# Unread bf16 products in TensorE's stream of a two-layer attention and expert kernel

## The reference, cut to what matters

```python
x = x + xattn_L0(layernorm(x), ctx)   # 16 heads of 8: causal self attention plus cross attention, projected
x = x + ffn_L0(layernorm(x))          # 8 experts of 128 -> 512 -> 128, relu, softmax over the best two
x = x + xattn_L1(layernorm(x), ctx)   # one head of 128, cross
x = x + ffn_L1(layernorm(x))          # 16 heads of 64; values and outputs mixed from the best two of 8 projections
```

## Time and profile before

| | |
|---|---|
| three runs, median | 1280.1 us (1278.98 to 1280.35) |
| profiled execution, its own time | 1274.52 us |
| its span, first to last instruction | 1272.8 us |
| mean granted TensorE clock over the span | 0.855 |
| instructions | 21333 |
| TensorE matmuls | 8499, busy 1118.9 us |

### The profile page before, as it was taken

How to read it: one execution, slowest core, us unless ns; L and a number is a source line. 1 busy time by engine, 2 the same in 40 slices (tenths; PEclk the granted TensorE clock), 3 DMA queues, 4 the chain that set the end, 5 groups by cost and what they waited for, 6 DMA issues and landing times.

```text
span 1272.8 us, 21333 instructions
## 1 busy us (share of the span) xinstructions
PE 1118.9 (88%) x8499; PEld 874.8 (69%) x8499; DVE 700.1 (55%) x1867; ACT 491.0 (39%) x1022; POOL 82.8 (7%) x246
## 2 busy tenths in 40 slices
PE   5888879899989998999989988998989998984696
PEld 4547645787569765887578855986678766873475
DVE  5503474856576565746575666657475657515400
ACT  4233406352434525352534434462536253422120
POOL 0020001000100001000100011000100010000000
PEclk8557958899889979898889978998889988998556
DMA  8000001051301421042103321052105220143322
GB/s 220 1 1 5 1 1 36 5 81 42 68 5 30 71 55 41 11 74 68 40 5 62 48 68 19 13 80 63 36 5 83 58 48 1 31 78 80 56 44 54
DMA packets 198033, 56.86 MB, mean 45 GB/s; under 512 B 173568, under 2 KB 193838, under 8 KB 197934
## 3 DMA queue, kind: packets, MB, share of 16 engines
q1 hardware_dynamic: 195630, 51.20, 20.6%
q10 hardware_dynamic: 2304, 4.29, 1.1%
HBM read 31.36 MB, written 24.12 MB: 44 GB/s over the span
## 4 chain that ended last, share of the span: by engine, by line
PE 74%; DVE 12%; ACT 7%; issue 2%; SPq 2%; DMA 2%; ACTq 0%; DVEq 0%
PE bank L737 10%; PE bank L928 10%; PE bank L773 9%; PE bank L843 5%; PE bank L884 5%; PE bank L663 4%; PE bank L624 3%; PE bank L678 3%; DVE negmax L1265 3%; PE bank L911 3%; ACT pa L1022 2%; PE bank L588 2%; PE bank L942 2%; ACT hi_part L1008 2%; PE bank L832 2%
## 5 line engine op out<-in xcount | busy, mean ns | idle before, releaser
L1265 DVE TENSOR_REDUCE negmax<-bank 128x2 f32<-128x512 f32 (+1 forms) x224 | 139.0, 683 | 57.2 <-PE bank L624 35.0
L1022 ACT ACTIVATE pa<-bank 128x512 f32<-128x512 f32 x224 | 123.4, 596 | 111.6 <-PE bank L678 73.7
L1039 ACT ACTIVATE pa<-bank,b_c 128x256 f32<-128x256 f32 x256 | 107.5, 471 | 117.9 <-PE bank L737 115.8
L737 PE MATMUL bank<-xnT_a,w 128*128 128x256 f32 x512 | 141.8, 429 | 0.1
L928 PEld LDWEIGHTS bank<-vb,pb 128*128 128x128 f32 x1024 | 129.6, 209 | 7.8 <-ACT pb L1101 3.0
L928 PE MATMUL bank<-vb,pb 128*128 128x65 f32 x1024 | 133.8, 294 | 1.2 <-ACT pb L1101 0.8
L773 PE MATMUL bank<-w,pa 128*128 128x128 f32 x1024 | 124.2, 276 | 0.0
L773 PEld LDWEIGHTS bank<-w,pa 128*128 128x128 f32 x1024 | 121.9, 192 | 3.2
L737 PEld LDWEIGHTS bank<-xnT_a,w 128*128 128x128 f32 x512 | 107.0, 219 | 18.4 <-ACT pa L1039 0.7
L1101 ACT ACTIVATE pb<-bank 128x512 f32<-128x512 f32 x128 | 69.8, 599 | 111.8 <-PE bank L888 110.9
L1419 DVE TENSOR_REDUCE negc<-bank 128x2 f32<-128x512 f32 x128 | 80.0, 684 | 46.4 <-PE bank L860 46.1
(11 more groups left out here) (239 smaller groups left out, 1690.5 us busy)
## 6 DMA issues: line engine op xcount, KB each, us to landing
v_d<-at SPq DMA_DIRECT2D x32, 256.0 KB, 3.3
vb<-v_d SPq DMA_DIRECT2D x32, 256.0 KB, 5.3
at_d<-at SPq DMA_DIRECT2D x32, 256.0 KB, 2.1
at<-at_d SPq DMA_DIRECT2D x32, 256.0 KB, 4.4
pv_d<-pvs SPq DMA_DIRECT2D x8, 512.0 KB, 2.8
pvs<-pv_d SPq DMA_DIRECT2D x16, 256.0 KB, 4.2
w<-in_L_ffn_W_dram ACTq DMA_DIRECT2D x1, 2048.0 KB, 10.5
bd<-mix_d SPq DMA_DIRECT2D x128, 8.0 KB
```

The lines of the kernel that those rows point to most:

```text
L737: mm = pe.matmul(BA[u % 2][:, c * T:(c + 1) * T], w1[:, e, f:f + P], xnT_a[:, :], start=True, stop=True)
L1022: nc.scalar.activation(pa[:, e % NPA, :], BA[e % 2][:, :], ACT.Exp, scale=SC0).then_inc(S["a_ex"], 1)
L1039: ins = nc.scalar.activation(hT[:, u % 4, c, :], BA[u % 2][:, c * T:(c + 1) * T], ACT.Relu, bias=b1_c[:, k:k + 1])
L1265: nc.vector.tensor_reduce(negmax[:, i:i + ng], BA[j][:, :].rearrange("p (g k) -> p g k", g=ng), AX, ALU.max, negate=True).then_inc(S["a_mx ...
```

## The change

TensorE gets 417 more products, of one form: half of the float32 identity, read as bf16, is the stationary operand, and the same half, repeated four times (512 columns), is the moving one. They write a PSUM bank that nobody reads before it is written again, have no semaphore and no wait, and are issued where the step list has a `w_` step. Six names differ only by bank and place:

- `w_first` (BB[3]), 175: one after `s_first`, the others before the a and c steps of sequence 0, by the counts of WARM_FIRST. A count that belongs to an f step is not used there, since those steps carry q = 1.
- `w_last` (BA[3]), 88: before the b steps of sequence 7, by WARM_LAST: 13 before `b_norm`, 7 before `b_norm_apply`, 3 before `b_gates`, 7 before `b_max` 0, and so on.
- `w_norm` (BA[0]), ten in each of the eight iterations: five before `c_kv`, five before `a_router`.
- `w_gather` (BB[0]), 31: five before `a_max` 6 in iterations 2 to 7, one before the last `b_norm`.
- `w_gates` (BB[0]), 43: one before `a_score` 1, four before `a_score` 2, one before `b_norm_apply`, one before `a_score` 3 in iterations 2 to 7 (together seven), one in iteration 1.
- `w_third` has no place.

So that BB[3] is free for `w_first`, the setup uses three banks instead of four: `s_cols` takes BB[1], `s_rows` BB[2], and `s_turn` BB[n % 3], waiting for the copy of step n - 3.

```diff
+        WARM_SETUP = 1
+        WARM_FIRST = [10, 4, 4, 14, 11, 7, 4, 9, 5, 6, 0, 13, 6, 3, 4, 3, 2, 2, 13, 0, 7, 0, 1, 6, 0, 3, 4, 5, 0, 0, 0, 0, 2, 1,
+                      3, 0, 1, 0, 0, 0, 2, 1, 2, 9, 11, 15, 4, 11, 0, 16, 14, 3, 6, 2, 10, 7]
+        WARM_LAST = [13, 7, 3, 3, 0, 0, 0, 5, 3, 2, 0, 0, 5, 1, 7, 3, 1, 2, 7, 2, 0, 4, 3, 0, 0, 0, 3, 4, 3, 1, 1, 1, 1, 0, 1,
+                      0, 0, 0, 0, 0, 0, 1, 1]
...
+        REGIONS = dict(w_norm=(("a_project", 0), ("a_router", 0)), w_third=(("a_expert", E - 1), ("c_q", 0)),
+                       w_gather=(("b_attend", 3), ("b_gather", 0)), w_gates=(("b_out", 0), ("b_gates", 0)))
+        KEPT = dict(w_norm={("c_kv", 0): 5, ("a_router", 0): 5},
+                    w_third={},
+                    w_gather={("a_max", 6): 5, ("b_norm", 0): 1},
+                    w_gates={("a_score", 1): 1, ("a_score", 2): 4, ("b_norm_apply", 0): 1, ("a_score", 3): 1})
+
+        def kept(order):
+            out, free = [], set()
+            for step in order:
+                for w, (opens, closes) in REGIONS.items():
+                    if step[:2] == closes:
+                        out += [(w, 0, step[2])] * (KEPT[w].get(closes, 0) if w in free else 0)
+                        free.discard(w)
+                    elif w in free:
+                        out += [(w, 0, step[2])] * KEPT[w].get(step[:2], 0)
+                out.append(step)
+                for w, (opens, closes) in REGIONS.items():
+                    if step[:2] == opens:
+                        free.add(w)
+            return out
...
-            order = [("f_load", 0, 0), ("s_first", 0, 0), ("f_norm", 0, 0), ("f_norm_apply", 0, 0), ("s_cols", 0, 0)]
+            order = [("f_load", 0, 0), ("s_first", 0, 0)] + [("w_first", 0, 0)] * WARM_SETUP
+            order += [("f_norm", 0, 0), ("f_norm_apply", 0, 0), ("s_cols", 0, 0)]
...
+                if q == 0 and (name, i) in STEPS_A:
+                    order += [("w_first", 0, 0)] * WARM_FIRST[STEPS_A.index((name, i))]
+                if q == B - 1 and name[0] == "b":
+                    order += [("w_last", 0, q)] * WARM_LAST[LAST_B.index((name, i))]
...
-            return order
+            return kept(order)
...
+                    def keep_busy(bank):
+                        half = ident[:, :].bitcast(BF16)[:, 0:P]
+                        pe.matmul(bank[:, :].rearrange("p (g k) -> p g k", g=4), half, half.unsqueeze(1).broadcast_to([P, 4, P]), start=True, stop=True,
+                                  skip_group_check=True)
+
+                    def w_first(_):
+                        keep_busy(BB[3])
...
-                        if n >= 4:
-                            pe.wait_ge(s_turnc, n - 3)
+                        if n >= 3:
+                            pe.wait_ge(s_turnc, n - 2)
                         for r, src in enumerate(turned_from[n]):
-                            mm = pe.transpose(BB[n % 4][:, r * P:(r + 1) * P], src, ident[:, :])
+                            mm = pe.transpose(BB[n % 3][:, r * P:(r + 1) * P], src, ident[:, :])
```

More of the change, by code:

```diff
@@ L380, in transformer_program @@
         assert len(LAST_AFTER) == len(LAST_B)
+        WARM_SETUP = 1
[3 more added lines that the diff above has]
+                      0, 0, 0, 0, 0, 0, 1, 1]
+        assert len(WARM_FIRST) == len(STEPS_A) and len(WARM_LAST) == len(LAST_B)
         def stream_b(q):
@@ L536, in s_first, with w_last, w_norm, w_third @@
                         mm.then_inc(s_turned_cols, 1)
+                    def keep_busy(bank):
[4 more added lines that the diff above has]
+                        keep_busy(BB[3])
+                    def w_last(_):
+                        keep_busy(BA[3])
+                    def w_norm(_):
+                        keep_busy(BA[0])
+                    def w_third(_):
+                        keep_busy(BA[1])
+                    def w_gather(_):
+                        keep_busy(BB[0])
+                    def w_gates(_):
+                        keep_busy(BB[0])
                     def s_cols(_):
                         pe.wait_ge(s_bspread, 3)
-                        pe.transpose(BB[3][:, 0:4 * G], bspread, ident[0:4 * G, 0:4 * G]).then_inc(s_turned_cols, 1)
+                        pe.transpose(BB[1][:, 0:4 * G], bspread, ident[0:4 * G, 0:4 * G]).then_inc(s_turned_cols, 1)
                         pe.wait_ge(s_spread, N_SPREAD)
@@ L545, in s_rows @@
                         for i in range(2):
-                            pe.matmul(BB[1][:, 3:4], brow[0:1, i, :], ones[0:1, 0:1], start=(i == 0), stop=(i == 1))
-                        pe.transpose(BB[1][:, 32:32 + E * FC], b1_rows, ident[0:E * FC, 0:E * FC])
-                        pe.transpose(BB[1][:, 96:98], bqk_rows, ident[0:2, 0:2]).then_inc(s_rows_done, 1)
+                            pe.matmul(BB[2][:, 3:4], brow[0:1, i, :], ones[0:1, 0:1], start=(i == 0), stop=(i == 1))
+                        pe.transpose(BB[2][:, 32:32 + E * FC], b1_rows, ident[0:E * FC, 0:E * FC])
+                        pe.transpose(BB[2][:, 96:98], bqk_rows, ident[0:2, 0:2]).then_inc(s_rows_done, 1)
                     def s_bias(_):
@@ L956, in b_out @@
                                     mm.then_inc(S["b_ro"], 1)
-                    own = dict(s_first=s_first, s_cols=s_cols, s_rows=s_rows, s_bias=s_bias, s_turn=s_turn,
+                    own = dict(s_first=s_first, w_first=w_first, w_last=w_last, w_norm=w_norm, w_third=w_third, w_gather=w_gather, w_gates=w_gates, s_cols=s_cols, s_rows=s_rows, s_bias=s_bias, s_turn=s_turn,
                                f_norm_apply=f_norm_apply, f_stack=f_stack, a_values=a_values, a_max=a_max, a_shift=a_shift,
@@ L1214, in s_cols @@
                         for kind in (Q0, QC):
-                            link(nc.vector.tensor_copy(bias_c[:, kind * G:(kind + 1) * G], BB[3][:, kind * G:(kind + 1) * G]), wait=False)
+                            link(nc.vector.tensor_copy(bias_c[:, kind * G:(kind + 1) * G], BB[1][:, kind * G:(kind + 1) * G]), wait=False)
                         for kind in (K0, KC):
-                            link(nc.vector.tensor_scalar(bias_c[:, kind * G:(kind + 1) * G], BB[3][:, kind * G:(kind + 1) * G],
+                            link(nc.vector.tensor_scalar(bias_c[:, kind * G:(kind + 1) * G], BB[1][:, kind * G:(kind + 1) * G],
                                                          shift_c[:, 0:1], None, ALU.add), wait=(kind == KC))
@@ L1227, in s_rows @@
                         dve.wait_ge(s_rows_done, 1)
-                        nc.vector.tensor_copy(bsum_c[:, :], BB[1][:, 3:4]).then_inc(s_rowc, 1)
-                        nc.vector.tensor_copy(b1_c[:, :], BB[1][:, 32:32 + E * FC]).then_inc(s_rowc, 1)
-                        nc.vector.tensor_copy(bqk_c[:, :], BB[1][:, 96:98]).then_inc(s_rowc, 1)
+                        nc.vector.tensor_copy(bsum_c[:, :], BB[2][:, 3:4]).then_inc(s_rowc, 1)
+                        nc.vector.tensor_copy(b1_c[:, :], BB[2][:, 32:32 + E * FC]).then_inc(s_rowc, 1)
+                        nc.vector.tensor_copy(bqk_c[:, :], BB[2][:, 96:98]).then_inc(s_rowc, 1)
                     def s_bias(_):
```

2 lines of the change are left out of this document (1 added, 1 removed).

## The result

The changed kernel takes 1237.4 us in the median of four runs (1229.6 to 1239.0), beside 1280.2 before: ratio 0.9674, interval 0.9648 to 0.9699, so 42 us off where 76 were forecast. The forecast of 1204 and its upper end of 1230 were too low; the sign was right.

What follows compares the result with a forecast made beforehand. It took TensorE, busy 88% of the span at a mean clock grant of 0.855, as the bound. Iteration 0's 11, iteration 1's 3, steady iterations' 40, the end's 21 and 1 make 76 off 1280.1: 1204, range 1189 to 1230.

Steps and rivals of the forecast that it cites:

- Price of a product: Each added 512-column product on TensorE was to cost 0.42 us at 1.2 GHz and 0.22 us at 2.4.
- The products hold the clock: Added products in TensorE's thin stretches were to raise the mean grant from 0.855 to about 0.94.
- the slower rival: Whole kernel: the products do not hold the clock and cost 72 us, so about 1350; chance 0.03.
- The end: Last sequence's b steps: mixes, scores and attention were to run at 2.4 GHz, 21 us off.
- Iteration 0: First iteration, with the w_first products: 11 us off, 8.6 of it from a_score 4 to a_heads.
- Iteration 1: Second iteration, with only the norm's ten products and one more: 3 us off, its score stage staying low.
- Gates: Value, gate, score and turn work of each steady iteration, with seven added products: 2.4 us off net.
- Norm: From c_kv to router and hidden layer of each steady iteration, with ten products: 3.1 us off net.
- Gather: Gather in each steady iteration, with five products before a_max 6: at most 2.1 us off, 1.5 taken.
- The gather of sequence 6: Near the last b_norm: a short fall of the clock at 1119 was to give 1 us.
- The rival of the half absorbed gain: Whole kernel: the clock rises but maxima, exponentials and transfer absorb half; 46 us off, 1234; chance 0.13.
- The page that disagreed: Whole kernel: by the page's under-1% rule the change could win at most 12.7 us, time 1267 or above.

Runs made afterwards that it cites:

- e1: The changed kernel with ten products instead of one before b_attend 0 of the last sequence: 1221.4 us, ratio 0.9558.
- e6: e1 with 28 of the 175 start products removed (before a_score 2 and 9, c_kv, a_expert 2, 3 and 5): 1219.4 us, ratio 0.9563.
- e10: e5 and e6 joined, with 26 products before the last b_norm, 28 before the last b_gather, three before a_max 5, four before a_max 6: 1212.6 us.
- e5: The changed kernel with the last sequence's b_sel behind b_mix 1 instead of ahead of b_mix 0, same number of products: 1221.0 us, ratio 0.9559.
- e3: The changed kernel with only the w_first products kept, all other added products removed: ratio 0.9972 to the kernel before.
- e9: e5 with b_max 2 and 3 of the steady iterations behind the router instead of in front of it: 1210.2 us, ratio 0.9474.
- e11: e10 with b_max 2 and 3 of the steady iterations behind the router, as in e9: 1206.3 us, ratio 0.9449.
- e2: The changed kernel with only the w_last products kept, all other added products removed: ratio 0.9825 to the kernel before.
- e12: e11 with every added product half as wide (256 columns instead of 512), same places and number: 1237.4 us, ratio 0.9694.

## Why the prediction was wrong, step by step

- **Price of a product**: right. Ten in front of the first `b_attend` of e1 take 2.17 us to the next instruction, 0.22 each.
- **The products hold the clock**: right in the main. 0.855 became 0.939 (forecast 0.94); the slower rival falls.
- **The end, 21 forecast, 3.4 found**: this is the step that failed: "After that the low stretch should end, because from 1178 TensorE has no gap of its own left." It did end, at 1172.1, but it was read from a trace in which slow scores hid the transfer of the values, and with fast scores TensorE has a gap of 2.04 us before the attention, in which the path goes through DMA. The 3.1 us expected from the scores were themselves what uncovered it. Nor does the lack of a gap bring the clock back: the earlier trace rows has 39.61 us busy of 41.40 at 0.50, and after the change the attention was busy 35.99 of 37.36 us and stayed low. The prediction had named this stretch at 0.5 as its sign of being wrong. With e1's bridge the end gives 3.4 + 15.8 = 19.2, so the size was nearly right and the condition missing. The fall expected at 1177 did not come: the last `b_split` waited 2.67 us where it had waited 5.81, and the clock held there.
- **Iteration 0, 11 forecast, 4.8 found**: `a_score` 4 to `a_heads` took 28.6 us (23.0 forecast). 3.4 us of it were still at low clock, and of the thirteens before `a_score` 2 and 9 a good part stood on the path (e6: 2.8 us off for 18 of the 26); e10, which has 28 products fewer, reaches the heads 3.7 us before e5. And a gain there does not last: e3 kept 1.1 of 4.2 at the end of the stream.
- **Iteration 1, 3 forecast, 2.5 found**: right in size by luck. The norm part, for which the 3 was meant, gave nothing; 1.9 came at the gates, where the low stretch ended at 192.5 instead of 201.1.
- **Gates, 2.4 forecast, 2.4 found** (1.7 in iteration 2, 2.6 in the others): right.
- **Norm, 3.1 forecast, 1.5 found**: the step "Sixteen hidden-layer records took 6.41 us where eight take 1.89 at 2.4, so 2.8 comes off" took the hidden products for the only thing late (and 6.41 less twice 1.89 is 2.6). `b_max` 2 and 3 ahead of the router and the logits cost 0.6 net, the falls that stayed another 1.2 in iterations 3, 5 and 7; some 0.3 is left, 0.2 of it the arithmetic.
- **Gather, 1.5 forecast, 0.8 found**: iterations 3, 5 and 7 kept a fall there (714.7 to 721.5) and gained 0.3 or nothing, 4 and 6 gained 1.6, iteration 2 0.8. "I take off 2 for falls that remain" was too little: two falls in every second iteration remained, and e9, with no fall between 196 and 1073 us, is 11 us faster than e5.
- **The gather of sequence 6, +1 forecast, 2.1 lost**: the 14 products at 2.4 GHz end at 1114.1, the transfer lands at 1118.5, and the clock falls in between. Before, the gather had run at half clock only in part. e10's 27 products cure it.
- **The range and the rivals**: the high side of the range adds up all its parts, the low side does not. The low ends named (4, 3, six times 5.0 less 2, 14, 1) make 50 us off, 1230 and not 1222. The measured 1237 lies beyond that too. The rival of the half absorbed gain (1234) comes nearest, but by luck: it leaves nothing at the gates, where 2.4 came, and 19 at the end, where 3.4 did.
- **The page that disagreed**: the Trainium skill (TensorE: Matmul & The Clock Gate, Part 1) puts the ramp penalty under 1% of a typical span. It says so of the products that a kernel issues before its clock first rises, and the prediction read it as a bound on everything that the clock costs. This kernel stood at half clock for 368 of its 1273 us, in 27 stretches. 42 us (3.3%) came off with the change itself and 5.5% with e11, so as such a bound it does not hold here.

## What to carry to other kernels

Filling TensorE's waits pays only where the steps behind them were held up by TensorE itself; read on every engine's queue who will be late next once it is fast, and above all which transfer a slow stage was hiding. The wait just before a long TensorE-bound stretch of small products is the one to fill or to remove, because here a fall there was paid for the whole stretch (2 us of products bought 16). Give the products about the length of the wait at full clock (halving them lost 31 us), and judge a local gain at the end of the program, since falls in later iterations can take it back.

## What was not expected of the hardware

- The same attention stood at either level to its end: 22.1 us at 1.00 in e1 and e5, 38.4 us at 0.50 before, and 37.4 us after, where the clock fell 1.9 us into it. By its rows TensorE was busy 36.0 of those 37.4 us, and the clock did not return.
- Executions of one kernel can differ by as much: e2 took 1254.4 to 1259.0 us in four runs and 1269.8 in one, with the attention at 0.50 in that one.
- Halving the width of the added products (e12) cost 31 of the 71 us that e11 had won.
- An edit that only moved two `b_max` steps behind the router (e9) took the clock from 0.954 to 0.970, with the same number of products.
